# A decoder with a mixture of experts on one core: the expert loop's matmuls in the order of experts, and the weights' rounding on GpSimd

## The reference, cut to what matters

```python
xl = x2 @ Wdown.T                                   # 2048 tokens, 64 latent features
probas = sigmoid(x2 @ Wg.T)                         # the best 8 of 16 experts get a weight, the others 0
...
shared = x2 @ sw1.T * sqrelu(x2 @ swg.T) @ sw2.T     # sqrelu(v) = relu(v) ** 2
acc = 0
for e in range(16):
    ye = xl @ rw1[e].T * sqrelu(xl @ rwg[e].T) @ rw2[e].T      # 64 -> 128 -> 64
    acc = acc + w_dense[:, e:e + 1] * ye
out = shared + acc @ Wup.T
```

## Time and profile before

| | us |
|---|---|
| median of three runs | 1028.16 |
| lowest, highest | 1028.05, 1029.35 |
| span of the profiled execution, first to last instruction | 1025.7 |
| the same execution's time outside its span | not given |
| TensorE, DVE, ACT, GpSimd busy in it | 973.5, 753.1, 744.1, 351.9 |
| expert loop, first gate product to last down product | 919.18 to 1011.00 |

### The profile page before, as it was taken

One profiled execution on the slowest core, in us unless ns is written; L12 is line 12 of the kernel. 1 busy time (PEld: TensorE's weight loads), 2 busy tenths in 40 slices (PEclk: granted clock), 3 DMA queues, 4 the chain that ended last, 5 costly groups with the idle time before them and its releaser, 6 DMA issues. The chain is left out here.

```text
span 1025.7 us, 19312 instructions
## 1 busy us (share of the span) xinstructions
PE 973.5 (95%) x6855; PEld 806.4 (79%) x6855; DVE 753.1 (73%) x1495; ACT 744.1 (73%) x2052; POOL 351.9 (34%) x306
## 2 busy tenths in 40 slices
PE   8899999999999999999998987889999999899997
PEld 4788888998899989988987876767778789774444
DVE  5888867667677676666757889879998644567774
ACT  5889877878778887777763348698999645558882
POOL 2242333333333333332320120266655310107672
PEclk9999999999999999999999998999999999999999
DMA  6321000000000001000205000000000000028652
GB/s 206 104 62 62 1 2 1 1 2 1 1 2 1 1 1 37 1 1 1 83 4 147 1 1 1 1 2 2 2 3 2 2 1 1 8 73 264 219 183 83
DMA packets 31840, 40.21 MB, mean 39 GB/s; under 512 B 8192, under 2 KB 23296, under 8 KB 31744
## 3 DMA queue, kind: packets, MB, share of 16 engines
q1 hardware_dynamic: 31744, 38.98, 12.2%
HBM read 36.74 MB, written 2.23 MB: 38 GB/s over the span
## 5 line engine op out<-in xcount | busy, mean ns | idle before, releaser
L354 POOL TENSOR_TENSOR roped_q<-roped_q,sin_q 128x512 f32<-128x512 f32 x64 | 81.8, 1279 | 270.6 <-DVE sin_q L518 270.6
L354 POOL TENSOR_TENSOR roped_k<-roped_k,sin_k 128x512 f32<-128x512 f32 x64 | 82.4, 1287 | 65.2 <-DVE sin_k L518 65.2
L1702 ACT ACTIVATE win_P<-banks,win_neg_max 128x128 f32<-128x128 f32 x256 | 91.3, 389 | 13.2 <-DVE win_neg_max L1789 13.0
L421 ACT ACTIVATE P<-banks,neg_max 128x128 f32<-128x128 f32 x256 | 90.1, 370 | 9.1 <-DVE neg_max L536 9.1
L464 ACT ACTIVATE oT_hi<-banks,bv_col 128x512 fp32r<-128x512 f32 x64 | 44.1, 689 | 58.0 <-PE banks L684 58.0
L1635 POOL TENSOR_TENSOR win_P<-win_P,win_inv 128x512 f32<-128x512 f32 x64 | 66.5, 1040 | 56.9 <-DVE win_inv L1794 56.8
L517 DVE SCALAR_TENSOR_TENSOR roped_k<-banks,qk_bias,cos 128x512 f32<-128x512 f32 x64 | 48.0, 750 | 51.3 <-ACT sin_k L430 51.0
L539 DVE SCALAR_TENSOR_TENSOR oT_lo<-banks,bv_col,oT_hi 128x512 fp32r<-128x512 f32 x64 | 47.9, 749 | 47.5 <-ACT oT_hi L464 47.5
L430 ACT ACTIVATE sin_q<-banks 64x512 f32<-64x512 f32 x128 | 75.9, 593 | 3.7 <-PE banks L37 1.4
L430 ACT ACTIVATE sin_k<-banks 64x512 f32<-64x512 f32 x128 | 75.8, 592 | 3.1 <-PE banks L37 0.8
L684 PE MATMUL banks<-PT,V 128*128 128x128 f32 x512 | 72.0, 284 | 5.6 <-ACT PT L448 5.5
(11 more groups left out here) (436 smaller groups left out, 3168.3 us busy)
## 6 DMA issues: line engine op xcount, KB each, us to landing
ret_V<-moe_gate_rows SPq DMA_DIRECT2D x16, 512.0 KB, 4.9
ctx<-moe_gate_rows SPq DMA_DIRECT2D x16, 512.0 KB, 5.1
X<-in_x SPq DMA_DIRECT2D x4, 512.0 KB, 6.4
stage<-in_wqT SPq DMA_DIRECT2D x4, 512.0 KB, 4.2
stage<-in_wvT SPq DMA_DIRECT2D x4, 512.0 KB, 6.2
stage<-in_woT SPq DMA_DIRECT2D x4, 512.0 KB, 4.3
ctx<-in_ctxT SPq DMA_DIRECT2D x4, 512.0 KB, 6.1
out<-X SPq DMA_DIRECT2D x8, 256.0 KB, 2.4
```

Source lines behind the costliest of these rows:

```text
L354: nc.gpsimd.tensor_tensor(roped[w][:, p, :], roped[w][:, p, :], sin_part[w][:], ALU.add).then_inc(roped_sum[w], 1)
L421: ins = nc.scalar.activation(P[:, i, :], SC[:, i * 128:(i + 1) * 128], ACT.Exp, bias=neg_max[:, r % 2, i:i + 1], accum_out=exp_sum[:, r % ...
L1702: ins = nc.scalar.activation(P[:, h % 2, s, i, :], SC[2 * (h % 2) + s][:, i * 128:(i + 1) * 128], ACT.Exp, bias=neg_max[:, h % 2, at:at + ...
```

## The change

TensorE's order in the loop goes by experts. For expert e: gate product of its first half; up product of the second half of the expert before; up product of its first half; gate product of its second half; then both down products of the expert before. GpSimd, not ACT, rounds the experts' weights: expert 0's after its one instruction before the loop, each later one ahead of the first multiply of the expert before it. DVE does gate_here ahead of both hiddens of a first half, not between them.

```diff
@@ block.gpsimd
+                def round_expert(e):
+                    pool.wait_ge(we_loaded[e % SLOTS], 64 * (e // SLOTS + 1))
+                    wait(pool, ups_done, NG + 2 * (e - 1) if e >= 2 else 0)
+                    nc.gpsimd.tensor_copy(we_hi[:, e % 2], we_in[:, e % SLOTS]).then_inc(we_rounded, 1)
+
+                round_expert(0)
                 for s in range(NG, STEPS):
+                    if s % NG == 0 and s // NG < E_:
+                        round_expert(s // NG)
                     if on_dve(s):
                         continue
@@ block.scalar
-                round_expert(0)
                 for s in range(NG):
...
                 for n in range(HALVES):
-                    if n % 2 == 0 and n // 2 + 1 < E_:
-                        round_expert(n // 2 + 1)
@@ block.vector
                         split_expert(n // 2 + 1)
-                    gate_hidden(s)
                     if on_dve(s + 1):
                         gate_here(s + 1)
+                    gate_hidden(s)
                     gate_hidden(s + 1)
@@ block.tensor
-                def up_pair(n):
...
+                def gate_up(n):
+                    if n % 2 == 0:
+                        pe.wait_ge(we_split, n // 2 + 1)
+                    if n == 0:
+                        pe.wait_ge(XL_ready, NG)
+                    pe.wait_ge(relu_done, NG + 2 * n)
+                    project_pair(n, 1, UG).then_inc(gate_ups_done, 1)
+
+                def up(n):
+                    s = NG + 2 * n
+                    pe.wait_ge(hidden_done, s - 2)
+                    project_pair(n, 0, U1[s % 4:s % 4 + 2]).then_inc(ups_done, 1)
...
-                for n in range(HALVES):
-                    up_pair(n)
-                    if n >= 2:
-                        down(n - 2)
+                for e in range(E_):
+                    gate_up(2 * e)
+                    if e > 0:
+                        up(2 * e - 1)
+                    up(2 * e)
+                    gate_up(2 * e + 1)
+                    if e > 0:
+                        down(2 * e - 2)
+                        down(2 * e - 1)
+                up(HALVES - 1)
                 down(HALVES - 2)
```

More of the change, by code:

```diff
@@ L2486, in square @@
                     nc.scalar.activation(squared[:, s % 4, :], relu[:, s % 4, :], ACT.Square).then_inc(square_done, 1)
[L2488 to L2491, removed]
                 normalise(2)
@@ L2670, in up_shared, with project_pair @@
                     project(up_bank(s), 1, s).then_inc(ups_done, 1)
-                def up_pair(n):
+                def project_pair(n, i, dst):
                     e, c = n // 2, n % 2
-                    s = NG + 2 * n
-                    if c == 0:
-                        pe.wait_ge(we_split, e + 1)
+                    for k, (weight, latent) in enumerate(((we_hi, XL_lo), (we_lo, XL_hi), (we_hi, XL_hi))):
+                        for half in range(2):
+                            rows = slice(half * LAT, (half + 1) * LAT)
+                            ins = nc.tensor.matmul(dst[half], weight[rows, e % 2, i, :], latent[rows, c, :], start=(k == 0), stop=(k == 2))
+                    return ins
+                def gate_up(n):
+                    if n % 2 == 0:
+                        pe.wait_ge(we_split, n // 2 + 1)
                     if n == 0:
                         pe.wait_ge(XL_ready, NG)
[L2679 to L2688, removed]
+                    pe.wait_ge(relu_done, NG + 2 * n)
[4 more added lines that the diff above has]
+                    project_pair(n, 0, U1[s % 4:s % 4 + 2]).then_inc(ups_done, 1)
                 def down(n):
```

## The result

The changed kernel takes 1020.32 us (median of 4 runs, 1019.32 to 1020.96), the kernel before on the same chip 1028.76 (4 runs, 1028.05 to 1029.4): ratio 0.9914, 95% interval 0.9901 to 0.9927, 8.4 us less. The forecast was 5.5 less. The direction was right, the gain half as large again, and more than the 8.0 us to which the forecast range reached (from 1028.16 down to 1020.2; the time itself, with a baseline 0.6 higher here, falls just inside). The time is that of the rival R2 (1020.4).

What follows compares the result with a forecast made beforehand. TensorE was taken as the bound, a GpSimd-DVE-TensorE loop just behind. Opening 0.3, twelve periods at 5.46 less 5.05, end 0.3: 5.5 us; span 1020.2, plus 2.46 carried over, gives 1022.7, range 1020.2 to 1027.2.

Steps and rivals of the forecast that it cites:

- R2: Rival, TensorE's floor: weight loads come ahead everywhere, or the split wins against multiply A0; 4.86 us per expert, 1020.4; chance 0.09.
- What bounded the kernel, and TensorE's part: Expert loop: TensorE bound, a GpSimd-DVE-TensorE loop just behind; fewer 64-row/128-row changes bring TensorE alone from 5.20 to 4.90 us.
- ACT: Expert loop: losing 15 of 16 roundings brings nothing by itself; relu just in time for gate B, 0.05 us charged.
- GpSimd: Expert loop: three multiplies and one CAST (0.40 us) take 4.3 us per expert, below 4.9, so its total is not the bound.
- The loop over DVE, the term that decides: Gate B through GpSimd multiplies, CAST, blocked split, gate_here and hiddens to up A: at least 4.95 us per expert, taken as 5.05.
- P: Time of one expert in the loop, two halves, gate A to gate A: 5.46 us before, forecast 5.05.
- The table: The prediction's start times along the DVE loop, counted from gate A: gate B 2.20, B0 4.95, up A released 11.39 us.
- the opening: First halves of the loop: gate of half 4 comes 1.2 us earlier, gate_here may give back about 1; 0.3 gained.
- End: From the last gate A to the last down: 10.06 us before, now 9.5 and 0.25 for waits; 0.3 gained.
- R1: Rival, the lost race: gate_here falls behind GpSimd's multiply B0, up A waits; mean 5.75 us per expert, about 1031.0; chance 0.10.
- R3: Rival, gain eaten: two downs save nothing, gate B late behind ACT, up A behind DVE; 5.35 us per expert, 1026.3; chance 0.11.
- R4: Rival: mode changes aren't the cost, TensorE merely waited under another name; stays 5.46 us per expert, 1027.6 to 1028; chance 0.04.

## Why the prediction was right in direction and short in size

**What bounded the kernel, and TensorE's part: right.** "TensorE alone: 4.84 to 4.99 us ... I take 4.90" measured 4.91; the twelve stages, 2.97 and the late 0.05, measured 3.04 (943.93 to 946.97); two downs measured 1.87, the lower of the two bounds. With the downs apart TensorE pays for the changes again.

**ACT: right.** Gate B is reached at 2.20, and the 0.05 charged is there (946.13 to 946.41 for a first stage that elsewhere takes 0.23). That the rounding had to leave its place in ACT's queue was not in the prediction as a condition, only as "nothing comes of it by itself"; the order with the old place costs 14.2 us over the changed kernel (1034.47 against 1020.32).

**GpSimd: right** in the CAST (0.39 to 0.41 long, next start 0.36 after), directly followed by a multiply.

**The step that failed: "The loop over DVE, the term that decides", with its end "With late weight loads I take P = 5.05".** The table's links and their order were right: split behind the lock, ending 0.28 to 0.29 after A0, gate_here 0.68, then two hiddens. (The split itself was to be 1.3 to 1.6 long and is 1.17; it comes later beside A0, 971.92 against 971.53.) Two sizes were wrong. The first is the loop. From gate B to up A the table had 9.19 (11.39 less 2.20), measured are 8.99. 0.11 of the 0.20 is the pair of multiplies: 1.31 each is the mean of a run of three (957.26 and 3.93), while the row of two in the same group has 2.54. The first of those three took 1.44; it started while gate_here was at work (timelines of 957 to 958 and of DVE):

```profile
957.26 1.44 POOL L2457 TENSOR_TENSOR moe_squared<-moe_squared,ctx 128x512 f32<-128x512 f32 x1 [1.19 <-ACT moe_squared L2486]
```

```profile
956.88 0.68 DVE L2561 TENSOR_TENSOR moe_squared<-moe_squared,ctx 128x512 f32<-128x512 f32 x1
```

The other runs of three without a collision take 3.90 or 3.91; in them the third starts late, 2.60 after the first (963.06, then 965.66), where the CAST here starts 2.51 after it. The gate-to-B0 link was 0.05 too long, A0 0.04. So P from the loop is 4.85, below TensorE's 4.91, and the maximum of two nearly equal numbers changed sides. The second size is the 0.10 on top, charged for a B0 held up by gate_here ("adds up to 0.2 per two experts") and for late weight loads. Neither was there in most experts: the pair of multiplies took 2.54 to 2.60 in all but one of the twelve (2.84), and up A stood 1.49 to 1.51 after gate A in all but one. Together 5.05 - 4.92 = 0.13 in each of 12 periods, 1.5 of the missing 2.9 us (8.45 less 5.5): 0.03 is the table's 4.95, 0.10 the charge.

**The second: the opening, "I count 0.3 gained", measured 1.58.** The gate of half 4 was to be 1.2 earlier, and is 1.40 earlier after the loop's start, and the period after it is 0.18 shorter than before; I took about 1 off for a multiply that would come ahead of gate_here. The race was run at 928.7, and gate_here won it by 0.03:

```profile
928.72 0.68 DVE L2562 TENSOR_TENSOR moe_squared<-moe_squared,ret_V 128x512 f32<-128x512 f32 x1
```

```profile
928.75 3.07 POOL L2466 TENSOR_TENSOR moe_squared<-moe_squared,ret_V 128x512 f32<-128x512 f32 x2 [0.24 <-ACT moe_squared L2495]
```

The multiply pays: two take 3.07 instead of 2.56. Other executions of the same kernel may have lost it; only this one was profiled, and the four times lie within 1.6 us. End: 0.43 for 0.3. The three differences, 1.5 + 1.3 + 0.1, are the missing 2.9.

**The rivals.** R2 came true (TensorE's floor), and of its two conditions the first: weight loads come ahead. The split did not win against A0. That its time fits to 0.1 us is in part luck: its P = 4.86 was 0.06 too short, 0.8 us too much gain in twelve periods, its 0.6 for both ends 1.4 too little (measured 1.58 + 0.43), and the kernel before had 1028.76 here, 0.6 above its starting point. R1 exists and is one swap or about one more microsecond on GpSimd away; its measured prices, 8.7 and 14.1 us over the changed kernel, hold the forecast of 1031 between them as times (1029.0 and 1034.4). R3 and R4 are ruled out by the period.

**The lock.** The eight-column split takes 1.24 us beside a multiply of 1.27, and the memset in its place 0.07: which DVE instruction waits is decided by whether it has two SBUF inputs, not by how much it moves. The trace agrees with the Trainium skill, "SBUF — State Buffer", section "Who interferes with whom", that such a pair blocks each other whole. What I drew from the lock was wrong: with it in full force the loop still fell below TensorE's time. It says who waits; how long the loop is had to come from rows without a collision in them.

## What to carry to other kernels

When two bounds are within a few per cent of each other, build each from rows that hold nothing of the wait that is added separately; a mean over a run of three in which a collision or a late start stands counts it twice, and can decide which bound you name. And a charge for a collision is only paid where the loop is the bound. Reordering one engine can need a queue of another rearranged before it pays: try the parts alone and together before judging any (here +8.6, +1.0 and -2.4 alone, -8.4 together). And find the distance to the nearest cliff by adding work on purpose: here 0.36 us was a slope, 1.08 us a cliff.

## What was not expected of the hardware

- The lock between DVE's two-input SBUF instructions and GpSimd's multiplies does not depend on width: 128x8 took 1.23 us in the mean of 14, as long as the multiply beside it, where a 128x8 memset took 0.065. Hiddens with one input in PSUM stayed at 0.69 beside multiplies in every kernel.
- The loser also pays when it comes second by little: two GpSimd multiplies take 2.66 to 3.07 us instead of 2.56 when gate_here stands in their way at the start (3.07 and 2.84 in the changed kernel, 2.90 to 2.95 with one more CAST, 2.66 to 2.69 with the narrow split).
- A DVE instruction of this shape that waits for the one before it on the same engine starts 0.76 or 0.77 after it instead of 0.60, in every expert of the kernel before.
- Two downs together take TensorE 1.87 us and 2 x 1.01 apart; with the ends of the 64-row stages, two more changes of tile form in an expert cost 0.29.
